# Down weights split once during the attention, three-term routed down products, and first projection pieces spread over token turns 7 to 16

## What is computed

```python
h = where(is_hot, hot_emb[tok2hot[ids]], cold_emb[tok2cold[ids]] @ proj.T)
h = h + attention(layernorm(h))     # causal, 16 heads of 32
x = layernorm(h)
p, e = top_k(softmax(x @ Wr.T + bias), 2)        # 16 experts, width 256
w = p / (sum(p) + 1e-9)
routed = sum_k w[k] * ((silu(x @ Wg[e[k]]) * (x @ Wu[e[k]])) @ Wd[e[k]])
shared = (silu(x @ sWg) * (x @ sWu)) @ sWd
out = h + routed + shared
```

## Time and profile before

| what | value |
|---|---|
| median of 3 runs | 969.42 us (968.51 to 969.42) |
| the profiled execution's own time | 968.75 us |
| its span, first to last instruction | 966.9 us |
| mean granted TensorE clock | 0.985 |
| busy: PE, DVE, ACT, POOL | 902.7, 657.3, 599.2, 444.8 us |
| token stage, about | 0 to 110 us |
| attention, about | 110 to 566 us |
| output projection, router and shared experts, about | 566 to 710 us |
| routed stage, about | 710 to 967 us |

### The profile page before, as it was taken

The page is one execution under the profiler, slowest core; times in us unless marked ns, Lnnn a source line. Parts: engine busy times, 40 slices in busy tenths (PEclk is TensorE's granted clock), DMA queues, the critical chain, the costliest instruction groups (busy, mean ns, idle before and its releaser), DMA issues.

```text
span 966.9 us, 21709 instructions
## 1 busy us (share of the span) xinstructions
PE 902.7 (93%) x6859; PEld 683.4 (71%) x6859; DVE 657.3 (68%) x1653; ACT 599.2 (62%) x1314; POOL 444.8 (46%) x494
## 2 busy tenths in 40 slices
PE   6779799999999999999997999999999999999995
PEld 5335578787887978878785677667766766676673
DVE  8895567576666757666675767768876666666662
ACT  6322487776768777777877833231156777777772
POOL 9377554533525346251500416633355476357332
PEclk9699899999999999999999999999999999999998
DMA  6135442323414143332313521261559478737430
GB/s 231 42 100 141 122 118 52 95 64 86 113 51 102 49 113 75 78 96 54 97 44 101 206 94 71 83 277 55 185 177 382 138 138 188 256 62 129 61 43 0
DMA packets 60513, 110.52 MB, mean 114 GB/s; under 512 B 15412, under 2 KB 21556, under 8 KB 58098
## 3 DMA queue, kind: packets, MB, share of 16 engines
q1 hardware_dynamic: 48082, 87.15, 29.1%
q0 software_dynamic: 12320, 21.99, 11.8%
HBM read 53.03 MB, written 25.17 MB: 81 GB/s over the span
## 4 chain that ended last, share of the span: by engine, by line
PE 76%; DVE 9%; issue 6%; SPq 4%; ACT 3%; POOL 1%; DMA 0%; DVEq 0%; POOLq 0%; ACTq 0%
PE psum L1563 13%; PE psum L692 11%; PE psum L1641 8%; PE psum L705 6%; PE psum L635 6%; PE psum L682 6%; PE psum L648 5%; PE psum L657 4%; SPq L450 4%; PE psum L1482 3%; PE psum L1595 2%; PE psum L1585 2%; PE psum L708 1%; DVE psum L821 1%; PE psum L1574 1%
## 5 line engine op out<-in xcount | busy, mean ns | idle before, releaser
L779 ACT ACTIVATE probs<-psum,nmax 128x128 f32<-128x128 f32 (+7 forms) x256 | 191.3, 747 | 37.4 <-DVE nmax L821 35.1
L821 DVE CUSTOM_DVE_ANT_0 psum<-psum,mask_row 128x128 f32<-128x128 f32 (+7 forms) x256 | 192.2, 767 | 27.6 <-PE psum L682 26.4
L692 PE MATMUL psum<-ident,probs 128*128 128x128 f32 x1152 | 175.2, 276 | 12.5 <-ACT probs L779 5.6
L692 PEld LDWEIGHTS psum<-ident,probs 128*128 128x128 f32 x1152 | 134.4, 140 | 48.3 <-ACT probs L779 18.0
L764 ACT COPY probsT<-psum 128x512 f32<-128x512 f32 (+3 forms) x256 | 129.2, 505 | 33.1 <-PE psum L692 30.7
L1055 POOL DMA_INDIRECT out<-xnT,slot_out x47 | 80.0, 1703 | 102.6 <-DMA out<-xnT,slot_out 73.7
L487 POOL CAST part_hi<-full 128x512 fp32r<-128x512 f32 x28 | 17.1, 610 | 206.6 <-ACT full L552 160.8
L682 PE MATMUL psum<-k_low,q_stack 128*128 128x512 f32 (+2 forms) x256 | 105.1, 418 | 5.2 <-ACT probs L779 2.6
L836 DVE TENSOR_TENSOR attnT<-psum,z_rows 128x128 f32<-128x128 f32 x64 | 18.7, 292 | 111.6 <-ACT z_rows L786 111.6
L1641 PE MATMUL psum<-w_dn,gated_T 128*128 x188 | 88.6, 593 | 1.0 <-ACT gated_T L1118 1.0
L1405 DVE TENSOR_TENSOR w_lo<-w_gu,w_hi 128x1024 fp32r<-128x1024 f32 x48 | 58.7, 1225 | 39.1 <-ACT w_hi L1147 37.7
(11 more groups left out here) (278 smaller groups left out, 2118.8 us busy)
## 6 DMA issues: line engine op xcount, KB each, us to landing
w_gu<-in_wgu SPq DMA_DIRECT2D x16, 1024.0 KB, 6.8
q_stack<-part_hi SPq DMA_DIRECT2D x128, 64.0 KB, 2.0
q_stack<-part_lo SPq DMA_DIRECT2D x128, 64.0 KB, 2.0
w_dn<-in_wd SPq DMA_DIRECT2D x16, 512.0 KB, 9.3
out<-acc SPq DMA_DIRECT2D x17, 256.0 KB, 3.9
hot_all<-xn SPq DMA_DIRECT2D x4, 1024.0 KB, 8.3
h_scratch<-hot_all SPq DMA_DIRECT2D x16, 256.0 KB
k_low<-part_hi SPq DMA_DIRECT2D x64, 64.0 KB, 2.0
```

The costliest lines, as they stand in the source:

```text
L692: mm = pe.transpose(bank(4 + m % 2)[:, (j - 4 * k) * P:(j - 4 * k + 1) * P], probs[n % PSLOTS][:, j * P:(j + 1) * P], ident[:, :])
L779: act.activation(probs[n % PSLOTS][:, 0:(i + 1) * P], score_bank(n)[:, 0:(i + 1) * P], ACT.Exp, bias=nmax[:, n % 4:n % 4 + 1], scale=-1.0, ...
L821: dve.tensor_tensor_reduce(out=row, in0=row, in1=mask_row[:, (QT - 1 - i) * P:QT * P], scale=1.0, scalar=3.0e38, op0=ALU.add, op1=ALU.min, ...
```

## The change

Four things change together.

1. During the attention SP loads the down weights of each of the 16 experts into one of two buffers (`load_down`), POOL splits them into high and low parts and stores both to a scratch tensor in DRAM (`split_down`: one cast and one subtraction of 128x1024, one store of 1 MiB). The buffers lie where heads of groups 2 and 3 are written later, so DVE waits for the stores before it first writes these groups (`normalize`).
2. In the routed stage the down product takes six f32r products instead of two f32 ones. ACT casts the turned gated rows (`turn_high`) instead of copying them, and DVE makes the low part (`turn_low`).
3. An expert's load is now 1 MiB of gate/up and 1 MiB of down parts; the ring has 4 slots instead of 6, and the down parts of the ring's first round are loaded into the room of `acc` behind the output's stores, after every fourth one; SP waits for these stores, and before the last of these loads for the spare rows' store. On ACT the weight cast of tile j+2 is moved ahead of the scaling of tile j-1. The gathered rows get a room of their own, so that 14 gathers are issued before the output is stored, instead of 8.
4. The six pieces of the first projection move from token turns 7, 8, 9, 11, 12, 13 to 7, 8, 10, 12, 14, 16, and the four splits of projection weights move from POOL to ACT and DVE, turns 9 to 12.

The diff, cut to its core:

```diff
-WRING = 6
-EARLY_EXPERTS = 4
+WRING = 4
-FIRST_FILL = {7: 0, 8: 1, 9: 4, 11: 2, 12: 3, 13: 5}
+FIRST_FILL = {7: 0, 8: 1, 10: 4, 12: 2, 14: 3, 16: 5}
+FIRST_SPLIT = 9
+DN_BOTH = 14
+DN_FIRST = {1: (0, 1), 2: (4, 5), 3: (8, 9), 4: (12, 13), 5: (15,)}
+DN_SECOND = {1: (2, 3), 2: (6, 7), 3: (10, 11), 4: (14,)}
...
+        dn_dram = nc.dram_tensor("dn_scratch", [E, P, 4 * D], F32, kind="Internal").ap()
+        sb("first_heads_room", [P, 2 * T], F32, spare_ctx)
+        dn_part = sb("dn_part", [P, 2, 2, 2 * D], F32R, spare_ctx)
...
+        w_dn = sb("w_dn", [P, WRING, 4, D], F32R, ring_ctx)
-        w_dn = sb("w_dn", [P, WRING, 2, D])
-        x_rows = [half_cols(i, 0) for i in range(X_RING // 2)] + [acc[:, i, :] for i in range(X_RING // 2, NT)]
+        x_more = sb("x_more", [P, X_RING // 2, D])
+        x_rows = [half_cols(i, 0) for i in range(X_RING // 2)] + [x_more[:, i, :] for i in range(X_RING // 2)]
...
+        def dn_set(e):
+            return (e % 2, e // 2) if e < DN_BOTH else (1, DN_BOTH // 2 + e - DN_BOTH)
+
+        def load_down(sp, e):
+            s, n = dn_set(e)
+            if n:
+                sp.wait_ge(s_dnst[s], 16 * (n + 1))
+            sp.dma_start(dn_part[:, s, 1, :].bitcast(F32), a["wd"][e].rearrange("p k n -> p (k n)")
+                         ).then_inc(s_dnraw[s], 16)
+
+        def split_down(pool, e):
+            s, n = dn_set(e)
+            pool.wait_ge(s_dnraw[s], 16 * (n + 1))
+            passed(pool)
+            raw = dn_part[:, s, 1, :].bitcast(F32)
+            pool.tensor_copy(dn_part[:, s, 0, :], raw).then_inc(s_dnsp, 1)
+            pool.wait_ge(s_dnsp, 2 * e + 1)
+            pool.tensor_tensor(dn_part[:, s, 1, :], raw, dn_part[:, s, 0, :].bitcast(F32),
+                               ALU.subtract).then_inc(s_dnsp, 1)
+            pool.wait_ge(s_dnsp, 2 * e + 2)
+            passed(pool)
+            pool.dma_start(dn_dram[e], dn_part[:, s, :, :].rearrange("p a n -> p (a n)").bitcast(F32)
+                           ).then_inc(s_dnst[s], 16)
...
         def att_sp(sp):
...
                     load_wq(sp, u // 2 + 1)
+                for e in DN_FIRST.get(u, ()):
+                    load_down(sp, e)
                 sp.wait_ge(s_S, HEAD + (u - 1) * STEPS + NARROW)
                 for side in range(2):
                     stack_half(sp, u, side, 0)
+                for e in DN_SECOND.get(u, ()):
+                    load_down(sp, e)
...
         def att_pool(pool):
...
+                for e in DN_SECOND.get(u - 1, ()):
+                    split_down(pool, e)
                 split_part(pool, u, 0, 0)
...
                 split_part(pool, u, 0, 1)
+                early, late = (DN_FIRST.get(u, ()) + (None, None))[0:2]
+                if early is not None:
+                    split_down(pool, early)
                 split_part(pool, u, 1, 1)
+                if late is not None:
+                    split_down(pool, late)
...
             def normalize(u, b, i, g):
                 dve.wait_ge(s_ZR, HEAD + u * QT + i + 1)
+                if b == 0 and i == 0 and g == 2:
+                    dve.wait_ge(s_dnst[0], 16 * (DN_BOTH // 2 + 1))
+                if b == 0 and i == 0 and g == 3:
+                    dve.wait_ge(s_dnst[1], 16 * (E - DN_BOTH // 2 + 1))
...
-            def load(e):
+            def load_gate_up(e):
+                sp.dma_start(w_gu[:, e % WRING, :, :], a["wgu"][e]).then_inc(s_wl[e % WRING], 16)
+
+            def load_down_parts(e):
                 s = e % WRING
-                sp.dma_start(w_gu[:, s, :, :], a["wgu"][e]).then_inc(s_wl[s], 16)
-                sp.dma_start(w_dn[:, s, :, :], a["wd"][e]).then_inc(s_wl[s], 16)
+                sp.dma_start(w_dn[:, s, :, :].rearrange("p k n -> p (k n)").bitcast(F32), dn_dram[e]
+                             ).then_inc(s_wl[s], 16)
...
             for c in range(NT):
                 store(c)
-                if c == NT // 2:
+                if c == NT - 1:
+                    sp.dma_start(out[T:T + P, :], acc[:, NT - 1, :]).then_inc(s_pad, 16)
+                    sp.wait_ge(s_pad, 16)
+                if c % (NT // WRING) == NT // WRING - 1:
                     sp.wait_ge(s_out, 16 * (c + 1))
-                    for e in range(EARLY_EXPERTS, WRING):
-                        load(e)
-
-            sp.dma_start(out[T:T + P, :], acc[:, NT - 1, :]).then_inc(s_pad, 16)
...
+                    load_down_parts(c // (NT // WRING))
             sp.wait_ge(s_plan, PLANNED)
             for e in range(WRING, E):
                 done = sp.value_load(tiles_to_i[0:1, e - WRING:e - WRING + 1], min_val=0, max_val=TILES)
                 sp.wait_ge(s_y, done + SHARED)
-                load(e)
+                load_gate_up(e)
+                load_down_parts(e)
                 if e > WRING:
                     ready(e - 1)
...
-            for j in range(X_RING // 2):
+            pool.wait_ge(s_wslo, NT)
+            passed(pool)
+            for j in range(GATHER_AHEAD):
                 gather(j)
...
             for j in range(TILES):
                 if j >= 1:
-                    turn_copy(SHARED + j - 1, (j - 1) % 2)
+                    turn_high(SHARED + j - 1)
                 weight_high(j + 1, 1)
                 silu(SHARED + j, j % 2)
                 row_high(j + 2)
+                weight_high(j + 2, 0)
                 if j >= 1:
                     y_scale(j - 1)
-                weight_high(j + 2, 0)
...
             for j in range(TILES):
+                if j >= 1:
+                    turn_low(SHARED + j - 1)
                 weight_low(j + 1, 1)
...
                 pe.wait_ge(s_gC, SHARED + j + 1)
+                if j < WRING:
+                    pe.wait_ge(s_wl[j], 32)
...
                 for k in range(2):
-                    mm = pe.matmul(bank(6 + p), gated_T[:, p, k * P:(k + 1) * P],
-                                   w_dn[:, bass.ds(half, 1), k, :].rearrange("p o n -> p (o n)"), start=(k == 0),
-                                   stop=(k == 1))
+                    for t, (g, part) in enumerate(((gs_hi, 0), (gs_lo, 0), (gs_hi, 2))):
+                        mm = pe.matmul(bank(6 + p), g[:, p, k * P:(k + 1) * P],
+                                       w_dn[:, bass.ds(half, 1), part + k, :].rearrange("p o n -> p (o n)"),
+                                       start=(k == 0 and t == 0), stop=(k == 1 and t == 2))
...
-                if 9 <= c < 9 + KC:
-                    split_weights_in(pool, 1, c - 9)
...
+                if FIRST_SPLIT <= c < FIRST_SPLIT + KC:
+                    first_weights_high(act, c - FIRST_SPLIT)
...
-                if c in FIRST_FILL:
+                if c in FIRST_FILL and c < NT:
                     first_low(dve, c)
                 if c < NT:
                     embed(c)
                 if c >= 1:
                     norm(c - 1)
+                if FIRST_SPLIT <= c < FIRST_SPLIT + KC:
+                    first_weights_low(dve, c - FIRST_SPLIT)
...
+            first_low(dve, NT)
```

More of the change, by code:

```diff
@@ L161, in build @@
         ring_ctx.close()
+        spare_ctx = ExitStack()
+        sb("first_heads_room", [P, 2 * T], F32, spare_ctx)
+        dn_part = sb("dn_part", [P, 2, 2, 2 * D], F32R, spare_ctx)
+        spare_ctx.close()
         attnT = sb("attnT", [P, GROUPS * T])
@@ L187, in build @@
         att_ctx.close()
+        ring_ctx = ExitStack()
+        w_dn = sb("w_dn", [P, WRING, 4, D], F32R, ring_ctx)
+        ring_ctx.close()
         acc = sb("acc", [P, NT, D])
@@ L321, in build @@
         s_wl = [sem(f"expert_loaded{i}") for i in range(WRING)]
+        s_dnraw = [sem(f"down_weights_loaded{i}") for i in range(2)]
+        s_dnsp = sem("down_weights_split")
         s_wr = sem("expert_weights_ready")
@@ L377, in build @@
         s_coldg = [sem(f"cold_gathered{i}") for i in range(NT)]
+        s_dnst = s_coldg[0:2]
         s_coldT = sem("cold_turned")
@@ L528, in split_weights_in, with first_weights_high, first_weights_low @@
             pool.tensor_tensor(wq_lo[:, c, :], src, wq_hi[:, c, :].bitcast(F32), ALU.subtract).then_inc(s_wqlo, 1)
+        def first_weights_high(act, k):
+            if k == 0:
+                act.wait_ge(s_wq, 16)
+            act.copy(wq_hi[:, k, :], w_unit[:, k, 0:2 * P]).then_inc(s_wqhi, 1)
+        def first_weights_low(dve, k):
+            dve.wait_ge(s_wqhi, k + 1)
+            dve.tensor_tensor(wq_lo[:, k, :], w_unit[:, k, 0:2 * P], wq_hi[:, k, :].bitcast(F32),
+                              ALU.subtract).then_inc(s_wqlo, 1)
         def att_pool(pool):
@@ L939, in moe_sp @@
             sp.wait_ge(s_wslo, NT)
-            for e in range(EARLY_EXPERTS):
-                load(e)
-            for e in range(EARLY_EXPERTS):
-                ready(e)
+            for e in range(WRING):
+                load_gate_up(e)
+            for e in range(WRING):
+                sp.wait_ge(s_wl[e], 16)
+                sp.sem_inc(s_wr, 1)
+            for s in range(2):
```

(21 more changed lines are left out.)

8 lines of the change are left out of this document (4 added, 4 removed).

## The result

The changed kernel takes 994.62 us in the median of four runs (990.59 to 994.76), the kernel before 969.08 beside it: ratio 1.025, interval 1.0225 to 1.0275. It is slower, as forecast, but by 25.5 us where 9.6 were forecast, and the time lies above the range. The profiled execution took 990.59 us with a span of 988.8, against 968.75 and 966.9: 21.9 us of span to account for.

A forecast was written before the change was run, and what follows sets the result against it. PE was taken to bound the kernel, three quarters of the span. Terms -15.0 + 0.5 (last tile) + 24.4 - 2.0 + 1.5 = +9.4 on 968.75 gave 978.15; with 0.67 for the median, 979 us, range 963 to 991.

The forecast's parts named there:

- Down product: Routed stage: six f32r products take 1.40 us instead of 1.72, in each of 47 tiles, -15.0 us.
- rival C: Routed down product: the change does not speed PE as meant, six products take 1.64 us; total 990, chance 0.07.
- Ring of four: Routed stage: four slots and 2 MiB loads make one-tile experts wait for loads, +24.4 us (13.8 and 10.6).
- L: Routed stage: time from issue to landing of a 2 MiB expert load, taken as 10 us, bounded by 7.6 and 11.5.
- rival A: Routed stage: loads land as with empty queues, in 7.6 us; stalls 11.0 us, total 965, chance 0.17.
- the time behind a landing: Routed stage: weight cast, scaling, turned cast, subtraction, down product and handovers before the next tile starts, 4.3 us.
- Attention: Attention: POOL's added splits lengthen DVE's z_inv copies, a third of DVE being idle; +1.5 us, bounds 0 and 6.
- stacks that wait for GpSimd's stores: Attention: stackings waiting for POOL's stores, listed as a sign in the profile that the forecast is wrong; no size given.
- rival B: Attention: the waits of DVE's z_inv copies lie wholly on the path, +4.5 us; total 983, chance 0.08.
- Token stage: Token stage: moved projection pieces shorten PE's low-clock work from 108 to 115 us; -2.0 us, bounds 0 and -4.
- Shared stage: Shared stage: down parts load early and gathers go before the spare rows' store, but PE waits for neither; 0 us.
- the case with all costs high: Whole kernel: all costs at their high end, 994 us; left out of the forecast range.

The follow-up runs named there:

- e2: Changed kernel with both halves of the next tile's weights cast and subtracted behind the turned rows' cast and subtraction, loads untouched: 995.93 us.
- e8: Changed kernel with small turns of the identity on TensorE ahead of the five down products that wait longest: 993.88 us.
- e4: Changed kernel without loads, splits and stores of down weights in the attention; the routed stage loads the raw weights twice: 987.4 us.
- e6: Changed kernel with all 16 splits on GpSimd in the attention, but only the first two experts' loads and stores: 985.3 us.
- e9: Changed kernel with split-weight stores issued by SyncE behind a finished half of stackings, a pair's splits together, last experts spread over one more unit: 986.73 us.
- e13: Kernel before with only the token-stage part of the change: 965.28 us against 970.32, ratio 0.9942.
- e11: Changed kernel with gate/up loads issued early, apart from down parts, and loads of 1.5 MiB from expert 4 on (low part not loaded): 965.63 us.
- e5: Changed kernel with gate/up loads issued early, apart from down parts, and SyncE's order mended to wait for nothing ahead of a due load: 973.63 us.
- e12: Changed kernel with early separate gate/up loads, split-weight stores issued by SyncE, and a fifth gate/up slot: 969.45 us.

## Why the forecast was wrong

- **Down product, -15.0:** right. 1.40 us, tiles of 4.83 against 4.85; rival C (1.64) fell. Cast and low part are hidden except behind the last tile and in the stalls.
- **Ring of four, +24.4:** the mechanism, the places (tiles 4 to 6, 22 to 27) and the landing time were right: L was put at 10 and, counted like there from the issue of the gate/up MiB (0.4 us ahead of the down parts), measured 10.7 and 10.8 in the first run, 10.1, 8.4 and 10.3 in the second; rival A (7.6) fell with them. The term that failed is the time behind a landing, put at 4.3 us. It measured 6.2 in three stalls and 5.8 in two. Two things were missing from it: the clock, by which the down behind a stall takes 2.94 (2.5 in two) instead of 1.40, which is most of the difference; and VectorE's queue, in which the subtraction of the weights (1.0) and its handovers stand ahead of that of the turned gated rows, which with all handovers makes 3.3 us ahead of the down instead of the forecast's 2.9. Over the five stalls the difference is 8.8; the measured stalls, 33.2, exceed 24.4 by as much. That it comes back when either is mended is not shown: e2 pays for it in the other tiles, and in e8, with the clock mended, next to nothing came back. The forecast's 6.8 us for 2 MiB was worked out from a figure for transfers that GpSimd issues, and these are SyncE's; nothing in its sum hung on that.
- **Attention, +1.5:** wrong, 5.8 us in the profile (506.16 to 509.63 with 2.3 of gain in front), 6.6 against e4. The forecast looked at SyncE only for waits ("Cover 4 us") and put its one cost on the port. The stores' own traffic beside the second-half stackings was not in the sum at all, though it was written that this stacking is critical; TensorE waited 5.4 us for it. The sign it named, stacks that wait for GpSimd's stores, did not show: they ran beside them, and slower. The contention of z_inv is real (353 to 401 and 420 ns) and e6 shows that it costs next to nothing, so rival B fell; e9, with the stores elsewhere, gives most of the loss back. The port pair that the Trainium skill, page "SBUF — State Buffer", section "SBUF: two separate sides", tells of agrees with z_inv's spread (226 to 1521 ns); that its waits reach the end is not what e6 shows, and VectorE is busy only 37.30 of 57.60 us in the window above.
- **Token stage, -2.0:** right, 2.3 in the profile; e13 shows that it reaches the end.
- **Shared stage, 0:** right within half a us: tile 0 is 3.3 later where the last stacking is 3.5 later.
- **Range:** the upper bounds of the two large terms, 33.3 and 6, were both met in size: -15 + 0.5 + 33.3 - 2 + 6 = +22.8, against the span's 21.9. It was left out as "the case with all costs high". That 33.3 meets the measured 33.2 is luck: it stood for a landing of 11.5 us with 4.3 behind it, and 8.4 to 10.8 with some 6 were measured. The median lies another 4 us above the profiled execution, and where those went is open.

## What to carry to other kernels

A smaller ring is priced from issue to the next use, and what stands behind a landing counts on every engine in its queue order, with the clock that an idle TensorE comes back with (0.50 to 0.60 here). Splitting a slot's release and its readiness by part gave back two thirds of the stalls here; of the rest a quarter fewer bytes took off two thirds (e11), and the other orders of waits that were tried (e5, e12) moved time to the end of the kernel. Precomputed data costs its bytes twice, where they are stored and where they are loaded: look for what critical small transfers stand beside the store.

## What the runs showed of the hardware that was not expected

- SyncE's groups of four 64 KB stacking transfers take 2.49 us in most cases and 3.4 to 3.8 beside a 1 MiB store that GpSimd issued, 4.02 beside one of SyncE's own. Most of what the attention lost lies there, and no engine's busy time shows it.
- The granted clock was 0.50 (1.2 GHz) in the 2.8 us after a stall in which TensorE had done nothing since 735.7, and 1.00 in e8, where it did small turns. The downs behind the five stalls took 5.5 us less with it, the routed stage 1.9 and the median 0.7.
- With the stalls gone the end came late instead: in e5 and e12 GpSimd's adds end 16.9 and 12.7 us behind the last down product, 9.8 in the kernel before and the changed one. In e11, with the shortest routed stage and a quarter fewer bytes, it is 9.8 again.
